# Table loads at the start of a macaron Mamba block: scale, zero and LoRA rows first, without clearing

## The reference

```python
def _L0_ffn_ref(x, qweight, scales, zeros, lora_A, lora_B, bias):
    W = (q - zeros[:, :, None]) * scales[:, :, None]    # q: 512 x 512 integers, groups of 64 columns
    y = jnp.einsum('bsi,oi->bso', x, W)
    lora = jnp.einsum('bsr,or->bso', jnp.einsum('bsi,ri->bsr', x, lora_A), lora_B)   # rank 16
    return y + 1/16 * lora + bias

x = x + 0.5 * _L0_ffn_ref(_layernorm(x), ...)
x = x + _L0_attn_ref(_layernorm(x), ...)     # h = x' + mamba2(rmsnorm(x')); h + silu(h2 @ gate) * (h2 @ up) @ down
x = x + 0.5 * _L0_ffn_ref(_layernorm(x), ...)
```

## Time and profile before

| quantity | value |
|---|---|
| median of three executions | 803.88 us (803.01 to 805.76) |
| the profiled execution | 802.2 us, of which the profile's span 800.5 us |
| TensorE matmuls busy | 762.1 us, 95% of the span |
| VectorE, ScalarE, GpSimd busy | 79%, 54%, 41% |
| mean granted TensorE clock | 0.991 of full speed |
| first product of the strip loop | starts at 45.91 us |

### The profile page before, as it was taken

How to read it: one execution, slowest core, us unless ns; L and a number is a source line. 1 busy time by engine, 2 the same in 40 slices (tenths; PEclk the granted TensorE clock), 3 DMA queues, 4 the chain that set the end, 5 groups by cost and what they waited for, 6 DMA issues and landing times.

```text
span 800.5 us, 10803 instructions
## 1 busy us (share of the span) xinstructions
PE 762.1 (95%) x3560; PEld 357.2 (45%) x3560; DVE 630.6 (79%) x1245; ACT 435.2 (54%) x853; POOL 324.8 (41%) x381
## 2 busy tenths in 40 slices
PE   7996899999999889999998999999999999999998
PEld 2442345455444444544443444444444444444443
DVE  4888878877886786786888897787887878757994
ACT  2675566767675566444544645546545645535441
POOL 4532353543442137486523214325225224223674
PEclk8999999999999999999999999999999999999999
DMA  8843543443341121421060263554544644344465
GB/s 305 201 81 65 106 79 75 84 93 66 66 79 41 27 40 40 106 50 30 1 158 14 53 145 61 106 128 73 127 102 81 140 83 77 68 84 72 114 164 132
DMA packets 98167, 72.41 MB, mean 90 GB/s; under 512 B 67984, under 2 KB 75152, under 8 KB 98112
## 3 DMA queue, kind: packets, MB, share of 16 engines
q0 software_dynamic: 17280, 31.46, 22.1%
q1 hardware_dynamic: 80448, 40.15, 19.7%
q10 hardware_dynamic: 384, 0.10, 0.1%
HBM read 20.32 MB, written 4.19 MB: 31 GB/s over the span
## 4 chain that ended last, share of the span: by engine, by line
PE 54%; DVE 5%; ACT 1%; issue 1%; DMA 0%; ACTq 0%; DVEq 0%
PE PS L1881 51%; PE PS L2009 1%; PE PS L1999 0%; DVE xds L1749 0%; DMA raw_gu<-raw_d 0%; DVE w_in L1488 0%; DVE xs L1824 0%; DVE st L1222 0%; DVE raw L1488 0%; DVE S L1747 0%; DVE mk L1415 0%; PE PS L2047 0%; DVE S L1817 0%; PE PS L1991 0%; PE PS L1982 0%
## 5 line engine op out<-in xcount | busy, mean ns | idle before, releaser
L691 POOL DMA_DIRECT2D xs<-x x59 | 51.6, 874 | 154.2 <-ACT x L1096 140.5
L1881 PE MATMUL PS<-h,w_in 128*128 128x512 f16 x480 | 108.9, 379 | 2.7 <-DMA h<-hn_p 1.4
L1881 PE MATMUL PS<-h,x_t 128*128 128x512 f16 x408 | 94.0, 379 | 0.0
L1881 PEld LDWEIGHTS PS<-h,w_in 128*128 128x128 f16 x480 | 46.6, 98 | 68.4 <-issue 15.3
L1881 PE MATMUL PS<-n_T,stage 128*128 128x512 f16 x288 | 71.8, 380 | 0.0
L503 POOL TENSOR_TENSOR r<-mv,mhalf 128x1 f32<-128x1 f32 (+1 forms) x32 | 28.3, 884 | 90.5 <-DVE mv L1226 70.8
L1096 ACT ACTIVATE x<-PS,d_d 128x512 f32<-128x512 f32 x59 | 40.2, 681 | 39.8 <-PE PS L1881 39.8
L1881 PEld LDWEIGHTS PS<-h,x_t 128*128 128x128 f16 x408 | 39.5, 98 | 48.5 <-issue 2.6
L691 POOL DMA_DIRECT2D xs<-n x29 | 25.5, 879 | 71.5 <-ACT n L1096 62.1
L1881 PE MATMUL PS<-pre,stage 128*128 128x512 f16 x192 | 49.3, 379 | 0.0
L1066 ACT ACTIVATE xds<-tm,dgh 128x512 f32<-128x512 f32 x24 | 17.3, 722 | 55.5 <-DVE tm L1812 55.5
(11 more groups left out here) (310 smaller groups left out, 1792.4 us busy)
## 6 DMA issues: line engine op xcount, KB each, us to landing
xs<-x POOLq DMA_DIRECT2D x75, 256.0 KB, 3.3
xs<-n POOLq DMA_DIRECT2D x29, 256.0 KB, 3.3
x_t<-x_in SPq DMA_DIRECT2D x16, 256.0 KB, 3.7
x_t<-hb POOLq DMA_DIRECT2D x16, 256.0 KB, 4.7
out<-x_t SPq DMA_DIRECT2D x16, 256.0 KB, 2.3
raw_gu<-gate_t SPq DMA_DIRECT2D x7, 512.0 KB, 4.5
raw_gu<-up_t SPq DMA_DIRECT2D x7, 512.0 KB, 6.4
raw_d<-down_t SPq DMA_DIRECT2D x7, 512.0 KB, 7.3
```

Source lines behind the costliest of these rows:

```text
L691: po.dma_start(chunk_of(xs, c), d_tmps[d % 3], accum_op=ALU.add).then_inc(s_acc[d % 3], 16)
L1881: ins = pe.matmul(out_, lhs(a, b, k), rhs(a, b, k), start=first and n == 0, stop=last and n == len(todo) - 1)
```

## The change

The scale and zero tables are issued first on SyncE's queue, ahead of x chunk 0. ScalarE's queue issues LoRA B and A with no wait ahead of them. The memsets of `sc` and of rows 32 to 127 of `sel_rows` go; that of `w_rows` shrinks to rows 0 to 31. The products take only the rows that hold something: 8 for the scale, 48 (K_W) for the other. `clear` moves from behind `w_in_bound` to between `zero_rows` and `ffn_weight(0)`.

```diff
@@ names
+        K_W = R_LORA + RANK
@@ sync
+            sp_.dma_start(sc[0:NG, :], scales_t).then_inc(s_la, 16)
+            sp_.dma_start(zt[0:NG, :], zeros_t).then_inc(s_la, 16)
             for k in range(KB):
                 load_x(k, k)
@@ gpsimd
-            po.memset(sel_rows[32:64, :], 0.0).then_inc(e_szero, 1)
-            po.memset(sel_rows[64:P, :], 0.0).then_inc(e_szero, 1)
@@ scalar
-            ac.wait_ge(e_wzero, 2)
-            ac.dma_start(sc[0:NG, :], scales_t).then_inc(s_la, 16)
-            ac.dma_start(zt[0:NG, :], zeros_t).then_inc(s_la, 16)
             ac.dma_start(w_rows[R_LORA:R_LORA + RANK, :], lora_b_t).then_inc(s_la, 16)
-            ac.wait_ge(e_szero, 2)
             ac.dma_start(sel_rows[R_LORA:R_LORA + RANK, :], lora_a).then_inc(s_la, 16)
@@ vector
-            ve.memset(sc[:, :], 0.0).then_inc(e_wzero, 1)
-            ve.memset(w_rows[:, :], 0.0).then_inc(e_wzero, 1)
+            ve.memset(w_rows[0:R_LORA, :], 0.0).then_inc(e_wzero, 1)
@@ zero_rows
-                ve.wait_ge(e_wzero, 2)
+                ve.wait_ge(e_wzero, 1)
@@ vector, order
             zero_rows()
+            clear()
             ffn_weight(0)
...
             w_in_bound()
-            clear()
             x1_stats(3, 3, B_P[1])
@@ ffn_parts
-                pe.matmul(bank(s_), sel_rows[:, cols], sc[:, :], start=True, stop=True)
+                pe.matmul(bank(s_), sel_rows[0:NG, cols], sc[0:NG, :], start=True, stop=True)
-                pe.matmul(bank(z), sel_rows[:, cols], w_rows[:, :], start=True, stop=True).then_inc(e_parts, 1)
+                pe.matmul(bank(z), sel_rows[0:K_W, cols], w_rows[0:K_W, :], start=True, stop=True).then_inc(e_parts, 1)
```

More of the change, by code:

```diff
@@ L257, in build @@
         e_max = sem("e_max"); e_maxT = sem("e_maxT"); e_max1 = sem("e_max1"); e_all = sem("e_all"); e_wsum = sem("e_wsum"); e_scale = sem("e_scale"); e_whi = sem("e_whi"); e_wlo = sem("e_wlo"); e_small = sem("e_small"); e_fhi = sem("e_fhi"); e_flo = sem("e_flo")
-        e_id = sem("e_id"); e_zero = sem("e_zero"); e_wzero = sem("e_wzero"); e_szero = sem("e_szero"); e_zs = sem("e_zs")
+        e_id = sem("e_id"); e_zero = sem("e_zero"); e_wzero = sem("e_wzero"); e_zs = sem("e_zs")
         e_aexp = sem("e_aexp"); e_sel = sem("e_sel"); e_wf = sem("e_wf"); e_dve = sem("e_dve"); e_pool = sem("e_pool")
```

## The result

The changed kernel takes 805.91 us in the median of seven executions (805.47 to 807.86) against 803.82 us for the kernel before on the same chip: 1.0039 of its time, 95% interval 1.0021 to 1.0058, or 2.1 us more. The forecast was 799.4 us. The profiled execution has a span of 804.2 us, 3.7 us more than before.

The account below looks back on a forecast made before the run. The prediction took TensorE's strip loop as the bound, so its start at 45.91 us decides. The weight chain gained 6.2 us, but the later bias chain left 4.5: 803.88 - 4.5 = 799.4 us, range 797.3 to 802.8.

Parts of the forecast that it names:

- The bound: Whole kernel: TensorE's strip loop fills the span; the gain is how much earlier than 45.91 us it starts.
- Table loads: Kernel start: LoRA A lands at 4.5 us, so the first product starts at 5.0 instead of 9.67 us, 4.7 us earlier.
- SyncE's issues: Kernel start: two extra issues on SyncE move x, q, `hb` and w_in back by about 0.8 us.
- Fewer rows: The eight weight products over 8 or 48 rows: effect taken as 0, at most 3.6 us less on their chain.
- the clock rival: Start: 8- and 48-row products don't hold TensorE's clock; loop 3 us later, 806.9 us; chance 0.08.
- Clock: Start: without the 4.68 us pause the clock stays at 1.00 after 4.6 us, products cost 0.9 instead of 1.7 us.
- The third rival: Start: thin products let the clock fall to 0.50 at about 8 us; loop 3 us later, 806.9 us; chance 0.08.
- `clear`: Moved ahead of `ffn_weight(0)`: hidden by TensorE but for nothing to 0.2 us; `x1_stats(3)` gains 1.0 us.
- Weight chain: Start, `ffn_weight` and `prep0` blocks: `first_f(0)` ends at 17.6 instead of 23.8 us, 6.2 us earlier.
- bias chain: Start, `hb` and the bias additions: 3.7 us earlier, `xb(1)` landing at 24.5 us; `w_in_bound` at 31.2, 4.5 us gain taken.
- sum: Whole kernel: the loop starts 4.5 us earlier, at 41.4 us, giving 799.4 us against the median 803.88.
- the last link: Strip loop to the end: the 4.5 us gained at the loop's start carries over whole to the kernel's time.

Follow-up runs that it names:

- e10_same_rows: e5_full_sp with all eight weight products over 48 rows, so none changes rows: 802.60 us, 0.9997 of the kernel before.
- e5_full_sp: Kernel before, its clearing and 128-row products kept, small tables issued early on SyncE, `zero_rows` ahead of `prep0(0)`, `clear` behind it: 801.24 us, 0.9970.
- e7_thin_sp: e5_full_sp with all eight weight products over 8 and 48 rows: 807.86 us, 1.0052 of the kernel before.
- e12_same_rows_again: Repeat of e10_same_rows, 48 rows in all eight weight products: 803.11 us, 0.9987 of the kernel before.
- e11_switch: e5_full_sp with a product of 8 rows and 8 columns behind each weight product: 800.69 us, 0.9970 of the kernel before.
- e4_clear_back: Changed kernel with `clear` put back behind `w_in_bound`: 807.85 us, 1.0046 of the kernel before.
- e8_long_warm: Kernel before with 30 junk products at the start instead of 9, loads still late: 803.52 us, 0.9997.
- e3_junk: Changed kernel, 8- and 48-row products kept, with thirteen full-row junk products put between them and ahead of waits: 810.41 us, 1.0091 of the kernel before.
- e6_thin_scale: e5_full_sp with only the four scale products cut to 8 rows: 807.39 us, 1.0047 of the kernel before.
- e1_thin: Kernel before with only the eight weight products cut to 8 and 48 rows, loads and clearing unchanged: 812.12 us, 1.0108.

## Why the prediction was wrong

*The bound.* Right for this pair: the start decides, and the rest moved with it (755.1 against 754.6 us behind the loop's first product).

*Table loads.* Right: first product at 5.02 us, forecast 5.0. *SyncE's issues.* `prep0(0)` began at 5.11 instead of the forecast 4.3, `zero_rows` at 6.15 against 5.4; small. `hb` was there before 11.60, not at 13.6: it landed 5.8 us after its issue instead of 8.0.

*Fewer rows.* This step failed in its price. I took 0 for the products and named 3.6 us of gain as the one bound beside the clock rival. They cost more, not less: 1.05 (6.88 to 7.93) instead of 0.86 us from one to the next at full clock (e10_same_rows), 2.00 instead of 1.7 at half, since each changes the rows used.

*Clock.* This step made the result wrong. "I expect the clock to stay at 1.00" took a busy engine for one that keeps its clock. e5_full_sp and e7_thin_sp differ in the rows of the eight products alone, and that puts 8.9 us of loop start on the rows, clock and switching together. e12_same_rows_again has 2.8 us of it with 48 rows and no switching, e11_switch 0.7 us with switching and full rows. The other 5.4 us came only with both, or with products over as few as 8 rows; these two were not parted. The third rival had it, with 0.08: 3 us later and 806.9 us, against 3.2 us and 805.91 measured. Its working priced `first_f(0)` at 7.2 us (measured 5.40, the clock came back inside it) and a product at 1.7 us (2.0), and the two misses nearly cancel: that it came so close is luck, its mechanism is not. I had put its chance low because the clock came back at 14.8 us before; but that was during products over all rows and said nothing of thin ones. A rival that no row speaks against, only the lack of a row, deserved more.

*`clear`.* Right in its new place: it ran from 6.78 to 7.74 us, and `ffn_weight(0)` still waited 0.40 us for TensorE. In its old place it did hold `x1_stats(3)` by the 1.0 us of the forecast, which was worth next to nothing at the loop (e4_clear_back).

*Weight chain, bias chain, sum.* Near for a kernel whose clock holds, though e5_full_sp issues its loads in another order than the one forecast. In e5_full_sp `first_f(0)` ended at 17.8 (forecast 17.6), `first_f(1)` started at 18.13 (18.5), `x1_stats(1)` at 24.11 behind the bias (24.5), `w_in_bound` released TensorE at 31.39 (31.2), the loop began at 41.98 (41.4). The forecast bias additions of 6.0 to 7.4 us were 7.0 and 7.3. Only the last link is weaker: 3.9 us at the loop gave 2.7 us between the medians, and 1.5 us in e8_long_warm gave nothing that can be told. Behind the loop's first product ten of the fourteen profiled executions took 754.6 to 756.4 us, the other four (e3_junk, e4_clear_back, e6_thin_scale, e8_long_warm) 757.9 to 760.0. Some of it lies in the first strips: a pause of 4.7 us there was followed by products at half clock in all thirteen traces that have it, shorter ones of 1.8 to 2.6 us in some and not in others. The executions of one kernel differ by 3 to 8 us (only e7_thin_sp's and the changed kernel's lie closer); whether that is the same thing is not shown, as one trace of each kernel is there, and what decides it was not tried.

## What to carry to other kernels

Cutting a product to the rows that hold data saved TensorE no time here, cost some where neighbours used other rows, and took the clock away from everything behind it; where zeros are to be had cheaply, keep the product over all rows, above all at the start. Don't count on work over few rows as warm-up, however busy the engine looks (18 us of it in e1_thin did not bring the clock back): read the granted clock and the duration of one product, not the busy share. When loads are made earlier, keep the clearing if it can be hidden, as e5_full_sp does, which is faster than both kernels here.

## What the runs showed of the hardware

- Rows of zeros count for the clock. The full products' extra rows hold only zeros, and they kept the clock where 48 rows (e10_same_rows, e12_same_rows_again) lost it at 11.7 us and 8 and 48 rows (e7_thin_sp) never got it before `first_f(0)`.
- A weight load ran beside the product before it when both used the same rows, 128 or 48, and did not begin before its end when the rows differed: 0.2 us more per product at full clock, 0.3 at half, where every product changes the rows. The Trainium skill ("TensorE: Matmul & The Clock Gate", Part 3: Packing small matmuls) says in one place that a weight load overlaps with products under way only when their row groups differ, and in another that it may also go to a background weight buffer. The overlap at equal rows (the load at 6.52 us) fits the second and not the first. For loads and products that start at the same row of the array, as all of these do (row 0), a change of the number of rows ended the overlap (the load at 7.37 us), and there the measurement decides.
- A product of 8 rows and 8 columns between full ones put their starts 0.5 us further apart (e11_switch) and did not lose the clock; products of 8 rows and 512 columns between full ones did not let it rise (e6_thin_scale).
